# First stage of a two-layer graph network: w split on three engines, a small band, x turned behind the first run; identity products taken out

## The reference

```python
x1 = relu(x @ W_ah + b_ah)
xs = [relu(gat_conv(x1, src, dst, W, a_s, a_d, b)) for each of 3 convolutions]   # 4 heads of 192
x  = layernorm(x + relu(concatenate(xs) @ W_out + b_out))                        # "x2" in the kernel
h  = elu(gat_layer(x, W1, 4 heads of 512))
x  = layernorm(x + gat_layer(h, W2, 1 head of 768))
```

## Time and profile before

| | us |
|---|---|
| median of 3 runs | 1923.69 |
| lowest, highest | 1923.25, 1928.69 |
| the profiled execution, time | 1930.16 |
| the profiled execution, span of its records | 1928.4 |
| its mean granted TensorE clock | 0.98 of full speed |

### The profile page before, as it was taken

One profiled execution on the slowest core, in us unless ns is written; L12 is line 12 of the kernel. 1 busy time (PEld: TensorE's weight loads), 2 busy tenths in 40 slices (PEclk: granted clock), 3 DMA queues, 4 the chain that ended last, 5 costly groups with the idle time before them and its releaser, 6 DMA issues. The chain is left out here.

```text
span 1928.4 us, 30682 instructions
## 1 busy us (share of the span) xinstructions
PE 1839.7 (95%) x11399; PEld 1776.6 (92%) x11399; DVE 1443.6 (75%) x2468; ACT 1030.9 (53%) x1634; POOL 142.1 (7%) x139
## 2 busy tenths in 40 slices
PE   7999999998999999998999999989999998999998
PEld 5877699998999999988999999989999998999997
DVE  8888599998888988965465549457888886346766
ACT  4676412218898889864211322257778875232632
POOL 5100211201000000000111011100000000000000
PEclk9999999999999999999999999989999999999989
DMA  4221335355455436619644466462342406544302
GB/s 126 67 64 54 99 103 149 101 133 142 134 111 131 108 77 149 145 16 248 185 141 143 135 208 188 141 193 79 108 143 66 138 28 204 156 129 126 99 9 80
DMA packets 179273, 234.12 MB, mean 121 GB/s; under 512 B 75943, under 2 KB 151655, under 8 KB 178889
## 3 DMA queue, kind: packets, MB, share of 16 engines
q1 hardware_dynamic: 170407, 202.98, 38.5%
q0 software_dynamic: 7984, 27.24, 4.9%
q10 hardware_dynamic: 748, 2.10, 0.4%
HBM read 167.27 MB, written 65.00 MB: 120 GB/s over the span
## 5 line engine op out<-in xcount | busy, mean ns | idle before, releaser
L1755 PE MATMUL p_o<-p_hi,h_parts 125*128 125x416 f32 (+1 forms) x960 | 283.0, 356 | 7.4 <-DVE z L1676 6.1
L1138 PE MATMUL p_o<-first_room,p 125*125 125x193 f32 x1200 | 202.2, 329 | 6.2 <-ACT res L1020 2.9
L1138 PEld LDWEIGHTS p_o<-first_room,p 125*125 125x125 f32 x1200 | 197.1, 189 | 8.0 <-issue 6.7
L1138 PE MATMUL p_o<-h_in,p 125*125 125x193 f32 x1200 | 200.9, 330 | 3.6 <-ACT res L1020 3.6
L1138 PEld LDWEIGHTS p_o<-h_in,p 125*125 125x125 f32 x1200 | 198.7, 190 | 5.0 <-issue 3.8
L1755 PEld LDWEIGHTS p_o<-p_hi,h_parts 125*128 125x128 f32 x960 | 182.0, 190 | 13.7 <-DVE z L1676 10.1
L781 DVE CUSTOM_DVE_ANT_0 max_junk<-src_row,G 125x1250 bf16<-125x1250 f32 x120 | 184.8, 1612 | 3.6 <-ACT src_row L819 1.5
L885 PE MATMUL p_h<-pw_hi,x1T 128*125 128x384 f32 x720 | 187.3, 341 | 0.0
L1088 DVE TENSOR_TENSOR e<-e 125x1250 f32<-125x1250 f32 x120 | 174.3, 1453 | 17.2 <-ACT e L1050 17.1
L1474 PE MATMUL p_h<-pw_hi,x2T 128*125 128x256 f32 (+1 forms) x960 | 177.8, 287 | 3.9 <-DVE h_out L1430 3.9
L1093 DVE SCALAR_TENSOR_TENSOR p<-e,CT 125x1250 f32<-125x1250 f32 x120 | 175.3, 1461 | 5.7 <-PE p_o L1138 1.7
(11 more groups left out here) (285 smaller groups left out, 3839.3 us busy)
## 6 DMA issues: line engine op xcount, KB each, us to landing
f_raw<-turned SPq DMA_DIRECT2D x40, 500.0 KB, 8.8
h_parts<-h_rows SPq DMA_DIRECT2D x40, 448.0 KB
turned<-tail_room SPq DMA_DIRECT2D x18, 625.0 KB, 6.9
G<-turned SPq DMA_DIRECT2D x20, 562.5 KB
h_rows<-tail_room SPq DMA_DIRECT2D x22, 424.4 KB
h_rows<-h_out SPq DMA_DIRECT2D x16, 560.0 KB
h_rows<-tail_room SPq DMA_DIRECT2D x14, 560.0 KB
first_room<-in_w_gat POOLq DMA_DIRECT2D x36, 192.0 KB, 2.7
```

The costliest lines, as they stand in the source:

```text
L1138: last = nc.tensor.matmul(p_o[:, b, n * 256:n * 256 + C0 + 1], p[:, g % RING, d * T:(d + 1) * T], h_in[hh][:, s, 0:C0 + 1], start=(s == 0 ...
L1755: last = nc.tensor.matmul(p_o[:, bank(n, c), 0:w], h[:, s, kind, cols].bitcast(F32R), pp[:, g % RING, 0:w], start=(s == 0 and j == 0), sto ...
```

## The change

- w's six pieces get six places in `G_room` and are loaded at once: three ahead of x and the bias, three behind. The split goes to three engines: ScalarE rounds and GpSimd subtracts the first three (`W_EARLY`), GpSimd rounds and VectorE subtracts the last three. TensorE waits for the first three before the first piece and for each of the others at its k.
- `band` has 376 columns in place of 2375; the identity products of the loop edges take their columns from it at other offsets.
- VectorE's reductions read the integer destinations; ScalarE makes the float copy. The sum `both` lies in PSUM in place of `meets[:, 0]` in SBUF. `before` is the constant 0 for tile 0, with no register load.
- The first run of tile 0 stands ahead of the loop over the runs, and x's first two groups are turned behind it, in place of ahead of the count. ScalarE makes its one-hots of that run first.
- `keep_busy` and its nine calls go, with the waits that stood ahead of two of them.
- In `project_layer1` three tiles are turned ahead of the products, VectorE's subtraction of w's unit 0 stands behind the rest of the first tile, the mean and variance are made at the beginning, the root between the first and second tile, and w's unit 1 is rounded ahead of the products.

```diff
+    W_EARLY = 3
-        band = sb("band", [T, 2 * N - T], BF16)
-        ident_b = band[:, N - T:N]
+        band = sb("band", [T, 3 * T + 1], BF16)
+        ident_b = band[:, T:2 * T]
@@ block.sync
-            dma_in_two(sp, x_in, rows_of(x)[:, 0:2, :], x_loaded)
-            sp.dma_start(bias[:], b_ah).then_inc(bias_in, 16)
             for k in range(KD):
-                if k >= 2:
-                    sp.wait_ge(w_split, 2 * (k - 1))
-                sp.dma_start(w_raw[:, k % 2, :], ...).then_inc(w_in[k % 2], 16)
+                if k == W_EARLY:
+                    dma_in_two(sp, x_in, rows_of(x)[:, 0:2, :], x_loaded)
+                    sp.dma_start(bias[:], b_ah).then_inc(bias_in, 16)
+                sp.dma_start(w_raw[:, k, :], ...).then_inc(w_in[k], 16)
@@ block.gpsimd
-            for k in range(KD):
-                pool.wait_ge(w_in[k % 2], 16 * (k // 2 + 1))
-                pool.tensor_copy(w_hi[:, k, :], w_raw[:, k % 2, :]).then_inc(w_split, 1)
-                pool.wait_ge(w_split, 2 * k + 1)
-                pool.tensor_tensor(w_lo[:, k, :], ..., ALU.subtract).then_inc(w_split, 1)
+            for k in range(W_EARLY):
+                pool.wait_ge(w_rounded, k + 1)
+                pool.tensor_tensor(w_lo[:, k, :], ..., ALU.subtract).then_inc(w_split, 1)
+            for k in range(W_EARLY, KD):
+                pool.wait_ge(w_in[k], 16)
+                pool.tensor_copy(w_hi[:, k, :], w_raw[:, k, :]).then_inc(w_rounded_late, 1)
@@ block.vector
-            step(v.tensor_copy(edge_f[:, 1, :], edge_i[:, 1, :]))
-            step(v.tensor_reduce(out=dst_ends[:, 0:1], in_=edge_f[:, 1, :], ...))
+            step(v.tensor_reduce(out=dst_ends[:, 0:1], in_=edge_i[:, 1, :], ...))
+            def rest_of_w(k):
+                dve.wait_ge(w_rounded_late, k - W_EARLY + 1)
+                v.tensor_tensor(w_lo[:, k, :], w_raw[:, k, :], ...).then_inc(w_split_late, 1)
                 rest_of_x(b, 1)
+                if b == 0:
+                    rest_of_w(W_EARLY)
                 rest_of_x(b, 2)
+                if b == 0:
+                    for k in range(W_EARLY + 1, KD):
+                        rest_of_w(k)
@@ block.scalar
+            for k in range(W_EARLY):
+                act.wait_ge(w_in[k], 16)
+                nc.scalar.activation(w_hi[:, k, :], w_raw[:, k, :], ACT.Copy).then_inc(w_rounded, 1)
+            now = first_hots(0)
+            act.wait_ge(bias_in, 16)
             round_x(0, 0)
             round_x(0, 1)
-            now = first_hots(0)
@@ block.tensor
-                with pe.Fori(0, count_) as j:
+                if t == 0:
+                    run(0)
+                    turn_x(0, 0)
+                    turn_x(0, 1)
+                with pe.Fori(0 if t else 1, count_) as j:
+                    run(j)
                 for k in range(KD):
+                    if b == g == m == 0 and k >= W_EARLY:
+                        pe.wait_ge(w_split_late, k - W_EARLY + 1)
-            keep_busy(nc, ident, p_count[:, 0, 0:128], 8)
@@ project_layer1
-    TURNED_FIRST = 2
+    TURNED_FIRST = X2_KEPT - 1
             round_w(0)
-            for i in range(TURNED_FIRST):
-                round_x(i)
+            round_x(0)
             act.wait_ge(var_done, 1)
             a.activation(root[:], var[:], ACT.Sqrt).then_inc(root_done, 1)
+            round_x(1)
+            round_x(2)
             act.wait_ge(ln_steps, 5)
             a.activation(x2_last, x2_last, ACT.Identity, ...).then_inc(normed, 1)
+            round_w(1)
@@ project_layer1, block.vector
-            dve.wait_ge(w_rounded, 1)
-            v.tensor_tensor(w_lo[:, 0, :, 0:HALF1], ...).then_inc(w_split, 1)
             for i in range(TURNED_FIRST):
                 rest_of_x(i)
+                if i == 1:
+                    normalization_goes_on()
                 if i == 0:
-                    normalization_goes_on()
+                    dve.wait_ge(w_rounded, 1)
+                    v.tensor_tensor(w_lo[:, 0, :, 0:HALF1], ...).then_inc(w_split, 1)
```

More of the change, by code:

```diff
@@ L94, in dma_in_two @@
         eng.dma_start(out[rows], in_[rows]).then_inc(sem, 16)
-def keep_busy(nc, ident, out, n):
-    for _ in range(n):
-        nc.tensor.matmul(out, ident[:, 0:out.shape[0]], ident[:], start=True, stop=True)
 class Chain:
@@ L165, in counts_and_x1 @@
         src_in = sem("src_in")
-        src_kept = sem("src_kept")
+        edges_kept = sem("edges_kept")
         ends_turned = sem("ends_turned")
-        w_in = [sem(f"w_in{i}") for i in range(2)]
+        w_in = [sem(f"w_in{k}") for k in range(KD)]
+        w_rounded = sem("w_rounded")
+        w_rounded_late = sem("w_rounded_late")
+        w_split_late = sem("w_split_late")
         bias_in = sem("bias_in")
@@ L274, in registers @@
                 count = dve.value_load(range_i[0:1, 1, bass.ds(t, 1)], min_val=LEAST, max_val=ER)
-                before = dve.value_load(range_i[0:1, 2, bass.ds(t, 1)], min_val=0, max_val=ER * NT)
+                before = dve.value_load(range_i[0:1, 2, bass.ds(t, 1)], min_val=0, max_val=ER * NT) if t else 0
                 return first, count, before
@@ L348, in registers @@
                 count = act.value_load(range_i[0:1, 1, bass.ds(t, 1)], min_val=LEAST, max_val=ER)
-                before = act.value_load(range_i[0:1, 2, bass.ds(t, 1)], min_val=0, max_val=ER * NT)
+                before = act.value_load(range_i[0:1, 2, bass.ds(t, 1)], min_val=0, max_val=ER * NT) if t else 0
                 return first, count, before
@@ L466, in count, with run @@
                 count_ = pe.value_load(range_i[0:1, 1, bass.ds(t, 1)], min_val=LEAST, max_val=ER)
-                before = pe.value_load(range_i[0:1, 2, bass.ds(t, 1)], min_val=0, max_val=ER * NT)
+                before = pe.value_load(range_i[0:1, 2, bass.ds(t, 1)], min_val=0, max_val=ER * NT) if t else 0
                 for i, (a, w) in enumerate(CH):
                     lo, hi = max(a, t * T), min(a + w, (t + 1) * T)
-                    lo, hi = (lo - a - (lo - a) % 2, hi - a + (hi - a) % 2) if lo < hi else (0, 2)
-                    nc.tensor.matmul(p_count[:, i, lo:hi], ident_b, band[:, N - T + a + lo - t * T:N - T + a + hi - t * T],
+                    at, to = (T + a - t * T, (lo - a - (lo - a) % 2, hi - a + (hi - a) % 2)) if lo < hi else (0, (0, 2))
+                    nc.tensor.matmul(p_count[:, i, to[0]:to[1]], ident_b, band[:, at + to[0]:at + to[1]],
                                      start=True, stop=False, skip_group_check=True)
-                with pe.Fori(0, count_) as j:
+                def run(j):
                     for h in range(RUN):
```

52 lines of the change are left out of this document (20 added, 32 removed).

## The result

| | before | after |
|---|---|---|
| median of 4 runs each, us | 1925.05 | 1911.91 |
| lowest, highest | 1923.25, 1928.69 | 1910.17, 1914.02 |
| the profiled execution: time, span | 1930.16, 1928.4 | 1911.75, 1910.1 |

A second set of 6 runs of the changed kernel gave 1911.21, ratio 0.9939 (0.9917 to 0.9962). The forecast was 1922.5, with a range from 1916 to 1928.5.

A forecast was written before the change was run, and what follows sets the result against it. TensorE, busy 95%, was taken as the bound, except up to about 31 us, where it waits for one-hots slowed by GpSimd. -3.65 + 0.9 + 2.0 - 0.3 = -1.05 us off 1923.69 gave 1922.5 (rounded), range 1916 to 1928.5.

The forecast's parts named there:

- First stage, -3.65: Start through x1 products: 5.4 us gained up to tile 0's count, less 1.75 for late parts of w.
- The first one-hot: First stage: it starts at 9.3 us, 2.6 us earlier than in the kernel before.
- The count: Tile 0 in the first stage: counting ends at 24.5 us instead of 30.1; a gain of 5.4 us was taken.
- The late parts of w: First x1 piece: k = 4 and 5 wait for VectorE's late subtractions, a loss of 1.75 us (1.2 to 2.9).
- Projection of layer 1, +0.9: Layer 1's projection: products start 1.6 us later, about 0.7 saved on turns, net loss 0.9 us (0 to 1.6).
- the fourth tile's copy: Layer 1's projection: ScalarE's earlier rounding delays this copy, not needed yet; uncovered it would cost 1.76 us at most.
- Identity products, +2.0 less 0.3: Nine places: without them low-clock restarts cost 2.0 us (0 to +11.5); 0.3 comes back in the first aggregation.
- 1.7 us for each of five falls: Stage starts without identity products: TensorE restarts at 1.2 GHz, losing 1.7 us of work each, up to 3.3.
- Every sign that I named for being right: One-hot near 9.3, tile 0 near 24.5, gap before k = 4, projection 1.6 us later, clock near 0.5 after three starts.
- Rival (a): Whole kernel: clearly faster, restarts cost nothing and the count speeds up early; -6.1 us, about 1917.5; chance 0.24.
- Rival (b): Whole kernel: slower, low clock after every stage start, five restarts at 3.3 us; +8.5, about 1931; chance 0.10.

The follow-up runs named there:

- f1: Changed kernel with all six pieces of w rounded and subtracted on GpSimd, TensorE waiting for all before x1; 1914.28 us, ratio to before 0.9950.
- f2: Changed kernel with the band of 2375 columns and the sum of the two comparisons back in SBUF; 1915.71 us, ratio to before 0.9961.
- a0: The changed kernel run again, unaltered; median 1911.21 us over 6 runs, ratio to before 0.9939.
- e2: Kernel before with only ScalarE's rounding of w's unit 1 moved ahead of the products of project_layer1; 1920.12 us, ratio 0.9981.
- a3: Changed kernel with two tiles turned first in project_layer1, as before, but the early rounding kept; 1909.05 us, ratio to before 0.9929.
- a4: Changed kernel with two tiles turned first and the early rounding kept, run again on another chip; 1914.34 us, ratio to before 0.9958.
- a1: Changed kernel with ScalarE's rounding of w's unit 1 back at the fifth tile; 1919.85 us, ratio to before 0.9976.
- e3: Kernel before with only the 88 identity products and the two waits ahead of two of them taken out; 1923.06 us, ratio 0.9987.
- a2: Changed kernel with all 88 identity products put back; 1914.43 us, ratio to before 0.9950.
- e4: Kernel before with only project_layer1 as in the changed kernel; 1923.56 us, ratio 0.9993.
- e1: Kernel before with only the changed first stage, its 8 identity products kept; 1918.29 us, ratio 0.9965.

## Why the prediction was wrong, step by step

**First stage, -3.65: right in the main, too small.** The first one-hot came at 9.26 for 9.3, tile 0 was counted at 24.3 for 24.5, and the last x1 product came 5.0 us earlier (medians of the profiles with either code, 215.5 and 210.5). The size was off in two terms. The count: the first x1 product, 30.9 to 32.7 in the four profiles of the old code (31.4), is at 24.2 to 25.2 in those of the new (24.5 in the middle), 6.9 us and not 5.4; 30.99 in the profile of before was at the early end, and between the two profiles it is 5.8. My reading of the rows behind this term was wrong in part: I took 4.75 us for twelve products and 4.62 for 24 as TensorE waiting for one-hots in both, but the first twelve ran at the low clock, and that the clock would rise earlier is in no term. The late parts of w stalled TensorE for 0.9 us, against 1.75:

```profile
PE p_x L543 <- DVE w_lo L305: 0.9, 2, 0.6
```

The first piece as a whole lost 1.4: its eighteenth product starts 3.43 us behind its first, in place of 2.04 (my 2.07 was a slip of small weight). Up to the last x1 product 1.9 us are given back (6.9 less 5.0), near the sum forecast for this, with only half of it in the wait that I named; f1 shows that it hangs on the split (1.7 back).

The Trainium skill, "SBUF — State Buffer", section "Who interferes with whom", says that a VectorE instruction with two SBUF inputs contends with a GpSimd instruction that reads SBUF, and one with at most one doesn't, outside the 2-port modes. The traces agree. In f2, beside GpSimd's fill and its subtraction, the two steps with both inputs in SBUF take 2.13 and 1.56 us. The changed kernel's 0.19 at 5.48 doesn't test the second half, as GpSimd stands idle there until 6.22; a0 does, where the subtraction runs beside the same step with one input in PSUM:

```profile
5.51 1.54 POOL L232 TENSOR_TENSOR w_lo<-G,w_hi 128x768 fp32r<-128x768 f32 x1 [1.18 <-ACT w_hi L348]
```

```profile
5.54 0.18 DVE L254 SCALAR_TENSOR_TENSOR G<-G,p_turn 10x40 f32<-10x40 int32 x1
```

**Projection of layer 1, +0.9: the step that failed most.** I wrote that ScalarE's earlier rounding delays the fourth tile's copy and that I count nothing else here. The 1.3 us to the first product are the reordering's: it comes 5.6 us after the first turn in every profile with three tiles turned first and 4.3 in e2, a3 and a4, which round early as well. Over the whole stage the three tiles cost about 0.5 (medians of the early-rounding profiles, 184.0 and 183.5), for +0.9. What I left out is who waits for the rounded unit: GpSimd's subtraction, behind it SyncE's mask load, behind it on the same queue the stores of h, behind them ScalarE, VectorE and TensorE. The stage measured -4.9 in the two profiles, -5.7 over all of them (medians 189.5 and 183.8), +6.7 when undone in a1 (190.6 and 183.8 in a0), and in whole runs -3.7 (e2) and +7.1 (a1). The kernel before had the row in its trace, a wait of 3.87 us of TensorE for VectorE at 1123.04 with 11.19 us of ScalarE for a store ahead of it, in a stage that I read only at its start.

**Identity products, +2.0 less 0.3: too high, and probably of the wrong sign.** Measured: -2.5 (e3, interval -5.0 to +0.2) and, put back, +2.1 (a2, with the wait of 2.13 us in it that isn't theirs by anything shown). That the gain is more than 0 is likely and not settled; a loss of 1.7 is outside e3's interval. The premise held: without them TensorE restarts at the low clock, 0.50 over the first 5.5, 5.4 and 3.8 us of products from 871.5, 1598.6 and 1784.5, where the kernel before has 1.00. I priced such a restart as lost work and let a later wait absorb some. What I didn't price is the other side, that a fast start can run into the next wait and lose the clock there. So does the start of the first output projection in some profiles. The timeline of e4, which has the identity products, then of e3, which hasn't:

```profile
876.25 0.54 PE L2013 MATMUL p_y<-fw_hi,f_hi 128*125 128x384 f32 x1 [0.53 <-DVE fw_lo L1936]
...
884.74 0.44 PE L2013 MATMUL p_y<-fw_hi,f_hi 128*125 128x384 f32 x1 [0.56 <-DVE fw_lo L1936]
...
889.35 0.44 PE L2013 MATMUL p_y<-fw_hi,f_hi 128*125 128x384 f32 x1 [3.29 <-DVE fw_lo L1936]
```

```profile
876.86 0.65 PE L2005 MATMUL p_y<-fw_hi,f_hi 128*125 128x384 f32 x1 [7.13 <-DVE fw_lo L1929]
```

e3 has one wait of 7.13 us and no later one over 0.4 until 900; e4 has three, and a low clock again from 890. e1 and e2 look like e4, with a fall at 883 and at 887; before and a2, which have the products as well, have no such fall, so this too is a part of the runs and not a rule. The Trainium skill, "TensorE: Matmul & The Clock Gate", Part 1, says the clock falls to half after an idle stretch and comes back after sustained work. The runs agree: the clock is at 0.50 behind the idle stretches named above and at 1.00 after it. What misled was the price that I put on it, 1.7 us for each of five falls: that would have been a loss, and e3 shows none.

**The sum.** Term by term: -5.0 for -3.65, -5.7 for +0.9, about -2.3 for +1.7, of which the last is the least certain. That makes -13.0, where whole runs gave -13.7 and, in the second set, -11.7. Of the 12 us between this and the forecast 6.6 are the queue, 4.0 the identity products and 1.4 the first stage. e1, e2 and e3 added make -12.9, each with 2.5 us to either side, so the near agreement is in part luck. Rival (a) had the right direction for the identity products and the count, but at -6.1 neither it nor another rival had the queue. Rival (b)'s time has a slip: +8.5 on 1923.69 is 1932, not 1931. Every sign that I named for being right came or nearly did, from the one-hot at 9.26 to the low clock at three stage starts; they tested what I had priced, and the term that failed had no sign.

## What to carry to other kernels

When an instruction is moved, follow its semaphore to every queue that waits for it, and then what stands behind that wait on the queue, to the end: here the last in the row was TensorE, 20 us behind the masks. Read the whole stage for waits of the bound engine, not its start alone. Don't count a slow start as a loss before you have read what follows it: where a wait follows, the wait can take up what the slow start loses, and a fast start can reach that wait and lose the clock behind it. Products that only keep the clock up weren't shown to pay here, over all nine places. And look at how long one product takes, not only at the printed clock: ahead of its first record the clock prints as full.

## What the runs showed of the hardware

From the first record of the clock to TensorE's last product the changed kernel has more time at the low clock than the one before, 81.9 us against 68.3 in the profiles (the stretch ahead of the first record, 16.8 and 23.3 us, would add to both), and is faster: at 857 to 877 the clock was low for 20.5 us, with TensorE busy for 10.2 of them. A mean granted clock tells little without what TensorE did in the low stretches. Falls of the clock come and go between executions of one kernel: stages with unchanged code differ by 2 to 4 us between profiles (the first projection, from the last x1 product, 213.4 to 217.3 in the nine without identity products), and medians of 4 and 6 runs of one kernel by 5 (a3 and a4), so that single parts of 2 us couldn't be settled by whole runs, but the 5.7 us of one stage could by its length over many profiles.
